# Turning each finished row block on VectorE in 32x32 transposes in place of fp32 matmuls

## What is computed

```
def layernorm(x): (x - mean(x)) / sqrt(var(x) + 1e-5)

def layer0(x, adj, u):
    keep = (u >= 0.1)
    return adj @ (x * keep / 0.9)

def layer1(x, adj, kernel, bias):
    x_proj  = tanh(|x|) * x / (|x| + 1e-8)          # |x| per node, clipped to 10
    support = adj @ x_proj
    out     = arctanh(|s|) * s / (|s| + 1e-8)       # s = support, |s| clipped to 0.999
    return out @ kernel + bias

x = layernorm(x + layer0(x, adj, u))
x = layernorm(x + layer1(x, adj, kernel, bias))
```

## Time and profile before

| | |
|---|---|
| time, median of 3 runs | 987.54 us (986.67 to 988.82) |
| span of the profiled execution | 983.9 us; its time with what lies around the span is not listed beside it |
| TensorE busy | 936.0 us, 3392 records |
| VectorE, ScalarE, GpSimd busy | 268.9, 53.4, 57.0 us |
| moved from HBM | 350.36 MB |

### The profile page before, as it was taken

One profiled execution on the slowest core, in us unless ns is written; L12 is line 12 of the kernel. 1 busy time (PEld: TensorE's weight loads), 2 busy tenths in 40 slices (PEclk: granted clock), 3 DMA queues, 4 the chain that ended last, 5 costly groups with the idle time before them and its releaser, 6 DMA issues.

```text
span 983.9 us, 8773 instructions
## 1 busy us (share of the span) xinstructions
PE 936.0 (95%) x3392; PEld 362.2 (37%) x3392; DVE 268.9 (27%) x886; ACT 53.4 (5%) x138; POOL 57.0 (6%) x49
## 2 busy tenths in 40 slices
PE   4678999999999999999999999999999999999994
PEld 1122333334343434343434444344343443434441
DVE  1120212214041312312131111301204013066775
ACT  0000000000000000000000000000000000002233
POOL 0000000000000000000000000000000000002332
PEclk9999999999999999999999999999999999999997
DMA  9999999998989899989599895997988989999980
GB/s 369 414 422 420 421 421 422 378 424 347 405 302 424 338 422 356 409 335 377 189 370 422 329 350 203 343 422 267 392 289 318 418 289 381 348 380 420 420 361 32
DMA packets 52743, 353.02 MB, mean 359 GB/s; under 512 B 6368, under 2 KB 8416, under 8 KB 10464
## 3 DMA queue, kind: packets, MB, share of 16 engines
q1 hardware_dynamic: 49824, 350.25, 89.5%
q10 hardware_dynamic: 2880, 2.23, 0.7%
HBM read 350.36 MB, written 2.10 MB: 358 GB/s over the span
## 4 chain that ended last, share of the span: by engine, by line
PE 81%; DMA 12%; SPq 3%; DVE 2%; ACT 1%; POOL 0%; issue 0%; ACTq 0%; POOLq 0%; DVEq 0%
PE sums_both L543 41%; PE sums_part L524 19%; PE sums_first L524 16%; DMA ring<-adj_dram 12%; PE turned L524 2%; SPq L283 2%; PE turned L575 1%; PE sums_both L585 1%; ACT xres L335 1%; PE sums_first L585 1%; SPq L278 1%; DVE stats L394 0%; POOL rooted L300 0%; DVE y L484 0%; SPq L279 0%
## 5 line engine op out<-in xcount | busy, mean ns | idle before, releaser
L543 PE MATMUL sums_both<-ring,feats 128*128 128x512 f32 x960 | 424.5, 597 | 2.3 <-DMA ring<-adj_dram 2.2
L524 PE MATMUL sums_first<-ring,feats 128*64 128x512 f32 x1088 | 249.0, 601 | 31.1 <-DMA ring<-adj_dram 31.0
L543 PEld LDWEIGHTS sums_both<-ring,feats 128*128 128x128 f32 x960 | 178.4, 190 | 238.0 <-issue 230.5
L524 PE MATMUL sums_part<-ring,feats 128*64 128x512 f32 x896 | 201.3, 596 | 0.0
L524 PEld LDWEIGHTS sums_first<-ring,feats 128*64 128x64 f32 x1088 | 75.8, 137 | 197.6 <-issue 137.3
L403 DVE TENSOR_TENSOR row_saved<-sums_both,row_saved 64x512 f32<-64x512 f32 x15 | 10.2, 683 | 389.7 <-ACT row_saved L351 389.7
L524 PEld LDWEIGHTS sums_part<-ring,feats 128*64 128x64 f32 x896 | 64.8, 136 | 130.6 <-issue 130.2
L441 DVE TENSOR_TENSOR support<-sums_part,support 64x512 f32<-64x512 f32 x86 | 58.8, 684 | 156.1 <-PE sums_part L524 156.0
L310 POOL TENSOR_TENSOR rooted<-base,power 128x8 f32<-128x8 f32 x16 | 27.8, 1738 | 842.2 <-DVE base L414 842.2
L442 DVE TENSOR_TENSOR support<-sums_part,support 64x512 f32<-64x512 f32 x87 | 60.4, 694 | 3.0
L351 ACT COPY row_saved<-sums_first 128x512 f32<-128x512 f32 x16 | 9.4, 587 | 725.4 <-PE sums_first L524 725.4
(11 more groups left out here) (54 smaller groups left out, 173.7 us busy)
## 6 DMA issues: line engine op xcount, KB each, us to landing
ring<-adj_dram SPq DMA_DIRECT2D x330, 1024.0 KB, 9.8
xres<-x_dram SPq DMA_DIRECT2D x8, 256.0 KB, 15.9
support<-u_dram SPq DMA_DIRECT2D x8, 256.0 KB, 16.0
out_dram<-xres ACTq DMA_DIRECT2D x16, 128.0 KB, 6.8
sel<-selector_dram ACTq DMA_DIRECT2D x1, 32.0 KB, 3.3
selw<-selector_dram ACTq DMA_DIRECT2D x1, 32.0 KB, 3.7
selw<-weight_dram ACTq DMA_DIRECT2D x1, 32.0 KB, 6.2
bias_sb<-bias_dram ACTq DMA_DIRECT2D x1, 32.0 KB, 6.6
```

Of the source, the lines that this page charges most:

```text
L524: last = nc.tensor.matmul(bank[at:at + F], feats[:, c * TB + t, which, :], ring[:, uses[i][0], t, :], start=start and t < 2, stop=stop and ...
L543: last = nc.tensor.matmul(sums_both[r % 2][:], feats[:, c * TB + t, :, :], ring[:, slot, t, :], start=c == 0 and t == 0, stop=c == r - 1 a ...
```

## The change

The matmuls of the turn go, with `sel`, its load and the two PSUM banks `turned`. ScalarE copies only the upper 64 partitions of `sums_first`. VectorE's join now makes the whole sum: the layer-0 half of `sums_both` plus the copied half, and then, in a second add, the lower half of `sums_first`; row 0 has a join too, of one add. At the turn step VectorE transposes in 8 instructions, each of 32 partitions x 4 tiles x 32 columns, from `row_saved` to an SBUF tile `turned`, and adds the residual from there. The freed banks give four banks to `sums_part` from the start. The waits that named the turn now name the join.

```
+PARTS = 4
+Q = 32
...
-        sel = sb("sel", [P, F])
+        row_sum, half_sum = row_saved[0:F], row_saved[F:P]
+        row_tiles = row_sum.rearrange("p (t n) -> p t n", n=P)
+        turned = sb("turned", [P, TB, F])
...
-        sums_part = [ps(f"sums_part{i}") for i in range(2)]
-        turned = [ps(f"turned{i}") for i in range(2)]
-
-        part_banks = sums_part + turned
+        sums_part = [ps(f"sums_part{i}") for i in range(PARTS)]
...
         @block.scalar
-            act.dma_start(sel[:], selector).then_inc(params_loaded, 16)
...
                     if r:
-                        act.wait_ge(row_turned, r)
-                    nc.scalar.copy(row_saved[:], sums_first[r % 2][:]).then_inc(row_sums_saved, 1)
+                        act.wait_ge(row_joined, r)
+                    nc.scalar.copy(half_sum[:], sums_first[r % 2][F:P]).then_inc(row_sums_saved, 1)
...
             def layer1_join(r):
 
-                dve.wait_ge(row_sums_saved, saved_through(r) - 1)
-                V.tensor_tensor(row_saved[0:F], sums_both[r % 2][0:F], row_saved[0:F], ALU.add).then_inc(row_joined, 1)
+                dve.wait_ge(row_sums_saved, 1 if r == 0 else saved_through(r) - 1)
+                if r:
+                    done(V.tensor_tensor(row_sum[:], sums_both[r % 2][0:F], half_sum[:], ALU.add))
+                    V.tensor_tensor(row_sum[:], sums_first[r % 2][0:F], row_sum[:], ALU.add).then_inc(row_joined, 1)
+                else:
+                    V.tensor_tensor(row_sum[:], sums_first[r % 2][0:F], half_sum[:], ALU.add).then_inc(row_joined, 1)
+                dve.wait_ge(row_joined, r + 1)
 
             def layer1_end(r):
                 rows = slice(r * TB, (r + 1) * TB)
                 own = slice(0, TB)
-                dve.wait_ge(row_turned, r + 1)
-                bank = turned[r % 2][:, 0:TB * F].rearrange("p (t f) -> p t f", f=F)
-                V.tensor_tensor(y[:, own, :], bank, xres[:, rows, :], ALU.add).then_inc(turned_read, 1)
-                dve.wait_ge(turned_read, r + 1)
+                for f in range(0, F, Q):
+                    for q in range(0, P, Q):
+                        last = V.transpose(turned[q:q + Q, :, f:f + Q], row_tiles[f:f + Q, :, q:q + Q])
+                done(last)
+                done(V.tensor_tensor(y[:, own, :], turned[:], xres[:, rows, :], ALU.add))
...
             def add_part(r, n, fresh):
-                total, bank = support[half(r), r // 2], part_banks[part_bank(n)[0]]
+                total, bank = support[half(r), r // 2], sums_part[n % PARTS]
...
         @block.tensor
                     if c == 0 and r >= 2:
                         pe.wait_ge(row_sums_saved, saved_through(r - 2))
-                        if r > 2:
-                            pe.wait_ge(row_joined, r - 2)
+                        pe.wait_ge(row_joined, r - 1)
...
                     if start and r >= 2:
-                        pe.wait_ge(row_sums_saved, saved_through(r - 2))
+                        pe.wait_ge(row_joined, r - 1)
...
-                    bank, before = part_bank(n)
-                    if start and before is not None:
-                        pe.wait_ge(part_added, before + 1)
-                    two_halves(part_banks[bank], 1, i, start, stop).then_inc(block_released, 1)
-                if kind == "turn":
-
-                    pe.wait_ge(row_sums_saved, saved_through(r))
-                    if r == 0:
-                        pe.wait_ge(params_loaded, 64)
-                    else:
-                        pe.wait_ge(row_joined, r)
-                    if r >= 2:
-                        pe.wait_ge(turned_read, r - 1)
-                    for t in range(TB):
-                        last = nc.tensor.matmul(turned[r % 2][:, t * F:(t + 1) * F], row_saved[:, t * P:(t + 1) * P],
-                                                sel[:], start=True, stop=True)
-                    last.then_inc(row_turned, 1)
+                    if start and n >= PARTS:
+                        pe.wait_ge(part_added, n - PARTS + 1)
+                    two_halves(sums_part[n % PARTS], 1, i, start, stop).then_inc(block_released, 1)
```

More of the change, by code:

```diff
@@ L163, in build @@
     groups = [s[1] for s in order if s[0] == "finish"]
[L165 to L175, removed]
     last_part = {s[1]: s[3] for s in order if s[0] == "part"}
@@ L238, in build @@
         row_joined = sem("row_joined")
-        row_turned = sem("row_turned")
         rows_projected = sem("rows_projected")
-        turned_read = sem("turned_read")
         projected_read = sem("projected_read")
@@ L430, in layer1_end @@
                 if r == 0:
-                    dve.wait_ge(params_loaded, 64)
+                    dve.wait_ge(params_loaded, 48)
                 done(V.tensor_tensor(xres[:, rows, :], xres[:, rows, :],
@@ L497, in _ @@
             for i, step in enumerate(order):
-                if step[0] == "hold" and step[2] == step[1] > 0:
+                if step[0] == "hold" and step[2] == step[1]:
                     layer1_join(step[1])
@@ L560, in _ @@
                     pe.wait_ge(mapped, c + 1)
-                    bank, before = part_bank(n)
-                    if start and before is not None:
-                        pe.wait_ge(part_added, before + 1)
-                    two_halves(part_banks[bank], 1, i, start, stop).then_inc(block_released, 1)
-                if kind == "turn":
-                    pe.wait_ge(row_sums_saved, saved_through(r))
-                    if r == 0:
-                        pe.wait_ge(params_loaded, 64)
-                    else:
-                        pe.wait_ge(row_joined, r)
-                    if r >= 2:
-                        pe.wait_ge(turned_read, r - 1)
-                    for t in range(TB):
-                        last = nc.tensor.matmul(turned[r % 2][:, t * F:(t + 1) * F], row_saved[:, t * P:(t + 1) * P],
-                                                sel[:], start=True, stop=True)
-                    last.then_inc(row_turned, 1)
+                    if start and n >= PARTS:
+                        pe.wait_ge(part_added, n - PARTS + 1)
+                    two_halves(sums_part[n % PARTS], 1, i, start, stop).then_inc(block_released, 1)
                 if kind == "finish":
                     rows = r
+                    if not finished:
+                        pe.wait_ge(params_loaded, 48)
                     pe.wait_ge(part_added, max(last_part[row] for row in rows) + 1)
```

## The result

The changed kernel takes 975.91 us (median of 4 runs, 973.91 to 977.76) against 987.16 us before (4 runs, 986.67 to 988.82). The ratio is 0.9884 with a 95% interval of 0.9867 to 0.99: 1.2% faster, and inside the predicted range of 975.0 to 983.5 us. The forecast was 978.7 us, a gain of 8.9 us; the profiled spans differ by 10.7 us (983.9 to 973.2). As a number that is a hit, 2.8 us above the measured time and with the result near the lower edge of the range. The parts behind it were not all right, and it was partly luck that they added up.

What follows compares the result with a forecast made beforehand. Memory was taken to bound the kernel up to 177.4 us and TensorE from there to the end of its stream. Twelve turns at 0.89 us saved, less 1.8 us lost in the last row, gave -8.9 us: 978.7 us, range 975.0 to 983.5.

Steps and rivals of the forecast that it cites:

- TensorE's time counts behind 177.4 us, not before: Whole kernel: memory sets the pace up to 177.4 us; TensorE time removed after that counts in full.
- rival B: Rows following 177.4 us: memory is the bound again, first five turns there give nothing; 983.1 us, chance 0.14.
- Rival C: Whole kernel: memory is the bound altogether, so no change; 987.5 us, chance 0.08.
- 0.89 us a turn, 10.7 us for 12: Rows 3 to 14: each turn removed from TensorE saves 0.89 us, 10.7 us for the 12.
- The banks at no cost and no gain: PSUM: four banks for partial sums cost nothing, and TensorE never waited for a bank.
- 8 transposes in 1.7 us: VectorE at each turn: transposes overlap and cost 0.21 us each, 1.7 us for 8.
- the nearer doubt: VectorE transposes: 0.29 us each, with no overlap, in place of the 0.21 us taken.
- A stall ahead of the last column, 1.8 us lost in place of 1.04 gained: Last row: mapped features come late, TensorE waits 2.6 us plus 0.2 us weight refill and starts the column 1.8 us later.
- In mid rows the features come earlier, and there is slack: Mid rows: residual add starts half a microsecond earlier; row 11 has 7.8 us of slack before TensorE needs the features.
- Rival D: Every row: transposes slow enough to stall TensorE, at 1.6 us each 37 us lost; 1024 us, chance 0.05.
- Rival A: Last turn: no stall, so all 13 turns are gained, 11.7 us; 975.8 us, chance 0.13.

Runs made afterwards that it cites:

- dummy_turn: Changed kernel with the turn's four matmuls back on TensorE in rows 1 to 15, result unused, three banks for partial sums: 986.76 us, ratio 0.9987.
- two_banks: Changed kernel with two banks for partial sums in place of four: 980.01 us, ratio 0.992.
- before_three: Kernel before, turns still on TensorE, with three banks for partial sums and one for turned rows: 984.22 us, ratio 0.9961.
- double: Changed kernel with each turn's 8 transposes done twice: 979.02 us, ratio 0.9918.
- again_two: Unchanged repeat of the changed kernel with two banks for partial sums in place of four, run for its clock trace: 981.42 us.
- turn_first: Changed kernel with the last turn put ahead of the first part after the last hold: 973.46 us, ratio 0.985.
- early_double: Changed kernel, last turn first after the last hold, seven blocks before the last column, first finish three blocks behind it, transposes done twice: 973.17 us, ratio 0.9853.

## Why the prediction was right, and where not

*TensorE's time counts behind 177.4 us, not before.* Right. Memory's waits stayed at 31 us, the stretch ahead of M didn't change, and no wait for the ring came back (rival B): behind the one of 0.6 us that ends at 177.4 us the list has none. Rival C is out: the mean over the span rose from 358 to 362 GB/s.

*0.89 us a turn, 10.7 us for 12.* Right: dummy_turn measures 10.6.

*The banks at no cost and no gain.* Wrong, the largest miss: "TensorE never waited for a bank" was read off the list of waits, and there a late weight load doesn't appear. It was 0.33 us in each of 12 columns, 4.0 us together; two_banks gives them back (3.9 us in M, 4.1 us in the medians) and before_three gets 3.8 us of M with the turn untouched. The sign was visible in the trace of before: weight loads of the third part out of their step of 0.43 us.

*8 transposes in 1.7 us.* Mis-sized: 2.51 us. They don't overlap; each starts 0.31 us after the one before (7 steps and 0.30 us). That is the value named as the nearer doubt. Overlap seen in one kind of instruction didn't carry to another. One difference stands in the code: the four statistics all write to the same partitions, and each transpose writes to another group of 32 partitions than the one before it. Whether that keeps them apart no run here tests. The Trainium skill's rule that the next operation waits for the pipe ("VectorE: DVE Perf Modes", "The DRAIN you can't avoid") gave an estimate of 2.3 us (8 x 0.29) and was nearer than the value I took from the statistics. The section also says "A next op that is not held starts earlier", which the prediction left out; the four statistics, 0.60 us together and 0.21 us for one alone, did start earlier.

*A stall ahead of the last column, 1.8 us lost in place of 1.04 gained.* The mechanism was right in each step, the size wasn't: L is 4.0 us longer. The idle time is 3.4 us against 2.6 predicted, 2.8 with the refill of weights. From the join to the end of the features it takes 11.1 us in place of 10.4, which is the transposes' 0.8 us, and TensorE goes on 0.1 us behind them in place of 0.2. Another 1.7 us are the clock, which the prediction left out. With the last turn's 1.04 us gained, 3.4 + 1.7 - 1.0 = 4.1 us.

*In mid rows the features come earlier, and there is slack.* Right where it matters: doubling all transposes costs M nothing. Rival D needed 1.19 us a transpose. (Against D it was said that no 512-element add takes over 0.69 us; one of 0.70 stands in the earlier trace rows, and nothing hangs on it.) By the trace of row 11 the residual add starts 4.7 us after the block (12, 0) has begun (601.25 - 596.54) and started 4.5 us after it before (610.74 - 606.24), so it is later by 0.2 us, not earlier by 0.6; the 0.8 us of the transposes again.

*Rival A* came closer in number (975.8 us) than the forecast, by luck: its mechanism was wrong, the stall was there and larger.

The sum as it should have been: -10.7 (turns) - 4.0 (banks) + 4.0 (last row) = -10.7 us, which is the difference of the spans. The forecast of 8.9 came out near because a missed gain of 4.0 us and missed losses of 2.2 us partly cancelled, which was luck.

## What to carry to other kernels

A freed resource is worth pricing by itself: here 4.0 of the 14.7 us gained ahead of the last row came from PSUM banks, and one of them could be had without the rest of the change. When TensorE has no waits in the list, look at the step of its weight loads before calling it free of waits. Where work moves from the busiest engine to an idle one, the row to look at is the one with the least cover, usually the last, and its stall costs more than its length when the clock falls behind it; the cheapest mend is order, not speed.

## What the runs showed of the hardware

- A 32-partition transpose of 128 fp32 elements on VectorE takes 302 ns, and 8 without a wait between them take 2.51 us, so one each 0.31 us. Four 64-element statistics, 0.21 us each alone, go through in 0.60 us.
- TensorE's granted clock fell from 2.4 to 1.2 GHz with an idle time of 3.4 us in four of five traces (the kernel after and two_banks together), with one of 5.9 us in double, and with one of 2.2 us in dummy_turn (0.89 in the mean of the 15 us around it). Mostly it fell behind the idle time; in again_two and double it fell within it. It stayed full behind 1.9 us (turn_first) and 1.1 us (early_double), and once behind 3.4 us (two_banks). The stretch cost 1.7 us of work in the kernel after.
- In the first 177 us TensorE waits for memory again and again. Ahead of its first matmul it waits 7.8 us, and after that no wait is over 2.0 us. The granted clock there is 1.00 in the kernel before, behind waits of up to 1.9 us. In the kernel after it fell once all the same: TensorE waited 2.0 us up to 18.0 us, and from 19 to 23 us the mean granted clock is 0.57. So waits of about 2 us went either way, as those of 3.4 us did. What decides it is open.
